# Quadrant attention: masked exponentials cleared on GpSimd, maxima transposed at once, queries and keys in one DMA

## The reference

```python
# layer 0: causal attention with a slope per head
q, k, v = split_heads(layernorm(x) @ W_attn + b_attn)            # 8 x 16 x 512 x 16
s = q @ k.T / (sqrt(16) * temperature) + slope[h] * (j - i)       # ALiBi
p = softmax(where(j <= i, s, -inf))
y = merge_heads(p @ v) @ W_proj + b_proj
# layer 3, second part: attention within sets of tokens, not causal (no mask by position)
p = softmax(q @ k.T / sqrt(16) + set_term(i, j)); y = merge_heads(p @ v) @ W_proj + b_proj
```

## Time and profile before

| | |
|---|---|
| median of 3 runs | 4843.05 us (4834.12 to 4845.9) |
| profiled execution | 4840.89 us, its span 4839.0 us |
| TensorE busy | 4549.0 us, 94% of the span |
| VectorE busy | 2544.5 us, 53% |
| ScalarE busy | 1674.0 us, 35% |
| GpSimd busy | 48.9 us, 1% |
| `score` of layer 0 (L316), 1024 instructions | 210.0 us |
| `score_t` of layer 0 (L323), 1024 | 233.4 us |
| exponentials of layer 0 (L399), 512 | 196.0 us |

### The profile page before, as it was taken

One profiled execution on the slowest core, in us unless ns is written; L12 is line 12 of the kernel. 1 busy time (PEld: TensorE's weight loads), 2 busy tenths in 40 slices (PEclk: granted clock), 3 DMA queues, 4 the chain that ended last, 5 costly groups with the idle time before them and its releaser, 6 DMA issues. The chain is left out here.

```text
span 4839.0 us, 58787 instructions
## 1 busy us (share of the span) xinstructions
PE 4549.0 (94%) x20997; PEld 2683.9 (55%) x20997; DVE 2544.5 (53%) x5867; ACT 1674.0 (35%) x3173; POOL 48.9 (1%) x36
## 2 busy tenths in 40 slices
PE   7999989999999999999999997999797896899997
PEld 3554546756666676666667665666465443333333
DVE  6666653242523325252332523887777776566764
ACT  3444432232222223223232322444342221355554
POOL 0000000000000000000000000000000000000000
PEclk9999999999999999999999998999998898899999
DMA  2000011111111111111111111000000000000001
GB/s 78 14 17 15 15 61 53 70 53 57 66 53 62 61 63 60 53 54 69 62 61 56 49 70 49 1 0 1 0 1 17 1 1 16 19 14 19 14 18 39
DMA packets 47767, 179.15 MB, mean 37 GB/s; under 512 B 12376, under 2 KB 20704, under 8 KB 30184
## 3 DMA queue, kind: packets, MB, share of 16 engines
q1 hardware_dynamic: 47488, 175.35, 10.5%
HBM read 152.76 MB, written 4.19 MB: 32 GB/s over the span
## 5 line engine op out<-in xcount | busy, mean ns | idle before, releaser
L1013 PE MATMUL l_exp_out<-l_w,l_hidden 128*128 128x256 f32 x4096 | 914.0, 384 | 0.3
L1003 PE MATMUL l_hid<-l_xn_t,l_w 128*128 128x512 f32 x2048 | 895.3, 595 | 15.3 <-ACT l_hidden L1132 15.3
L1013 PEld LDWEIGHTS l_exp_out<-l_w,l_hidden 128*128 128x128 f32 x4096 | 782.9, 193 | 118.6 <-issue 9.2
L1132 ACT ACTIVATE l_hidden<-l_hid,l_w 128x512 f32<-128x512 f32 x512 | 350.8, 687 | 1017.5 <-PE l_hid L1003 1017.5
L1003 PEld LDWEIGHTS l_hid<-l_xn_t,l_w 128*128 128x128 f32 x2048 | 390.2, 191 | 490.8 <-issue 466.4
L428 DVE TENSOR_REDUCE l3f_row_max<-l3f_bank 128x1 f32<-128x512 f32 x512 | 328.5, 685 | 178.2 <-PE l3f_bank L316 177.8
L1270 DVE SCALAR_TENSOR_TENSOR l_moe<-l_exp_out,l_gates,l_moe 128x256 f32<-128x256 f32 x256 | 123.6, 483 | 485.3 <-PE l_exp_out L1013 480.6
L399 ACT ACTIVATE l3f_prob_t<-l3f_bank 128x512 f32<-128x512 f32 x512 | 278.0, 595 | 275.3 <-PE l3f_bank L323 275.1
L323 PE MATMUL l3f_bank<-l3f_q_t,l3f_k_t 32*128 32x512 f32 x1024 | 313.8, 640 | 1.4 <-ACT l3f_prob_t L399 1.3
L425 DVE CUSTOM_DVE_ANT_0 l_masked<-l_bank,l_mask 128x384 f32<-128x384 f32 (+3 forms) x512 | 229.1, 488 | 161.0 <-PE l_bank L316 159.1
L316 PE MATMUL l3f_bank<-l3f_k_t,l3f_q_t 32*128 32x512 f32 x1024 | 301.6, 657 | 8.5 <-DMA l3f_q_t<-l3f_set_rows_q 7.4
(11 more groups left out here) (448 smaller groups left out, 6178.8 us busy)
## 6 DMA issues: line engine op xcount, KB each, us to landing
l_w<-in_w SPq DMA_DIRECT2D x128, 1024.0 KB, 5.0
all_x<-in_x SPq DMA_DIRECT2D x8, 512.0 KB, 11.0
l_q_t<-l_packed SPq DMA_DIRECT2D x128, 32.0 KB
l_k_t<-l_packed SPq DMA_DIRECT2D x128, 32.0 KB
l3f_q_t<-l3f_packed SPq DMA_DIRECT2D x128, 32.0 KB
l3f_k_t<-l3f_packed SPq DMA_DIRECT2D x128, 32.0 KB
out_x<-all_x SPq DMA_DIRECT2D x8, 512.0 KB, 5.7
l_hidden<-in_fp4w SPq DMA_DIRECT2D x1, 2304.0 KB
```

What stands on the lines that cost most here:

```text
L1003: ins = nc.tensor.matmul(bank[:, :], w1[:, e % 2, c, f * P:(f + 1) * P], xn_t[:, c, :], start=c == 0, stop=c == CT - 1)
L1013: ins = nc.tensor.matmul(bank[:, 0:C], hidden[:, e % 2, f, j * P:(j + 1) * P], w2[:, e % 2, f, :], start=f == 0, stop=f == HF - 1)
L1132: hid.empty(nc.scalar.activation(hidden[:, e % 2, f, :], bank[:, :], ACT.Relu, bias=w[:, B1][:, e * HF + f:e * HF + f + 1]), (e, f))
```

## The change

1. Layer 0 drops `diagonal`. GpSimd clears the masked exponentials in `prob_t` with `affine_select`, one instruction for two heads (256 elements per partition), two per step. `prob_t` gets a third buffer, and the values follow two steps later in layer 0 (LAG 2), still one in layer 3. So that no exponential above the diagonal grows too large, four spare rows of the slots (`halves`) add -1e30 where the query lies in the first half of a 128-block and the key in the second.
2. The maxima lie densely in `row_max`, so one transpose gives 16 rows of 128. ScalarE copies them, negated, into `max_rows`, and SP writes them into the `MAX_ROW` rows of `q_t` with four DMAs. `centre` is gone. AHEAD grows from 5 to 8; the transpose comes at t % 4 == 1 instead of 3.
3. `q_t` and `k_t` are one tensor `qk_t`, and one DMA per head moves both; the set rows of layer 3 likewise. SP now goes through the steps, with moves at i = 6, 8, 12 and 0 of the next.
4. Some work moves: the transposes of x from i = 3 to 2, the first query and key projections from 5 and 6 to 4 and 5, set rows from 2 to 3, in layer 0 the transposes and copies of y one step later and `yt` from 4 to 5.
5. In layer 3 the copy of the register tokens' queries is four plain copies, and the `channel` mask is gone. Clearing `row_max` at the start is gone in both.

The diff, cut to its core:

```diff
-    AHEAD = TJ + 1
+    AHEAD = 2 * TJ
...
+        self.causal, self.parts, self.flow, self.LAG = causal, parts, flow, 2 if causal else 1
+        self.qk_t = a.sb("qk_t", [P, 2, G, T])
+        self.q_t, self.k_t = self.qk_t[:, 0], self.qk_t[:, 1]
+        self.row_max, self.max_rows = a.sb("row_max", [P, 2, TJ * HPG]), a.sb("max_rows", [TJ * HPG, 2, P])
+        self.prob_t = a.sb("prob_t", [P, self.LAG + 1, HPG, T])
...
+    def move(self, sp, b, g):
+        u, first = g // 2, g % 2 * HPG
+        self.flow.wait_emptied(sp, ("q", b, u))
+        self.flow.wait_emptied(sp, ("k", b, u))
+        for s in range(HPG):
+            sp.dma_start(self.qk_t[s * SLOT:s * SLOT + D, :, g, :],
+                         self.packed[(first + s) * D:(first + s + 1) * D, :, u, :]).then_inc(self.moved[g], 16)
+
+    def move_maxima(self, sp, t):
+        g = self.group_of_maxima(t)
+        if g is not None:
+            self.flow.wait_emptied(sp, ("mx", g))
+            for qt in range(TJ):
+                sp.dma_start(self.q_t[self.MAX_ROW::SLOT, g % G, qt * P:(qt + 1) * P],
+                             self.max_rows[qt * HPG:(qt + 1) * HPG, g % 2, :]).then_inc(self.max_moved, 16)
...
-        qt = self.wave_order[i % TJ]
+        qt = TJ - 1 - (w - self.AHEAD) % TJ if self.causal else i % TJ
...
+    def group_of_maxima(self, t):
+        g, i = divmod(t + self.AHEAD - 1, TJ)
+        return g - 1 if i == 0 and 0 <= g - 1 < B * G else None
+
+    def group_of_sums(self, t):
+        g, i = divmod(t - self.LAG - TJ + 1, TJ)
+        return g if i == 0 and 0 <= g < B * G else None
...
             for s in range(HPG):
-                flow.wait_emptied(pe, ("t", u, s))
+                if not self.causal:
+                    flow.wait_emptied(pe, ("t", u, s))
+                elif s % 2 == 0:
+                    pe.wait_ge(self.selected, 2 * u + s // 2 + 1)
...
-            for j in range(TJ):
-                ins = nc.tensor.transpose(bank[:, j * P:(j + 1) * P], self.row_max[:, g % 2, j].rearrange("p s r -> p (s r)"), ident)
-            flow.fill(ins, ("mx", g))
+            flow.fill(nc.tensor.transpose(bank[0:TJ * HPG, 0:P], self.row_max[:, g % 2, :], ident), ("mx", g))
...
             if t % TJ == 0:
-                flow.wait_emptied(pe, ("mx", t // TJ))
+                pe.wait_ge(self.max_moved, 16 * TJ * (t // TJ + 1))
...
-        if 0 <= t < n:
-            diagonal(0)
-            diagonal(1)
-        if 0 <= t - 1 < n:
-            values(t - 1)
-        if t % TJ == TJ - 1 and 0 <= t + 1 < n:
-            maxima((t + 1) // TJ)
+        if 0 <= t - self.LAG < n:
+            values(t - self.LAG)
+        if self.group_of_maxima(t) is not None:
+            maxima(self.group_of_maxima(t))
...
-            diagonal(2)
-            diagonal(3)
...
+        g = self.group_of_maxima(t)
+        if g is not None:
+            if g >= 2:
+                act.wait_ge(self.max_moved, 16 * TJ * (g - 1))
+            bank = flow.wait_filled(act, ("mx", g))
+            flow.empty(nc.scalar.activation(self.max_rows[:, g % 2, :], bank[0:TJ * HPG, 0:P], ACT.Copy, scale=-1.0), ("mx", g))
...
+    def gpsimd(self, nc, pool, t):
+        for s in (0, 2):
+            for h in (s, s + 1):
+                self.flow.wait_emptied(pool, ("t", t, h))
+            block = self.prob_t[:, t % (self.LAG + 1), s:s + 2, 0:P]
+            nc.gpsimd.affine_select(block, block, [[0, 2], [1, P]], ALU.is_ge, 0.0, 0, -1).then_inc(self.selected, 1)
...
# layer 0, SP
+            sp.wait_ge(halves_ready, 1)
+            for s in range(HPG):
+                rows = slice(s * SLOT + att.MAX_ROW + 1, s * SLOT + att.MAX_ROW + 1 + TJ)
+                for g in range(G):
+                    sp.dma_start(att.qk_t[rows, :, g, :], halves).then_inc(halves_moved, 16)
             sp.dma_start(w[:, WK.stop:BQ.start], w_dram[:, WK.stop:BQ.start]).then_inc(w_loaded, 16)
             for b in range(FIRST, B):
                 load_x(sp, b)
+            for t in TIMES:
+                b, i = divmod(t, att.STEPS)
+                att.move_maxima(sp, t)
...
+                if i in MOVES:
+                    g = MOVES.index(i)
+                    tile = b + 1 if g < G - 1 else b
+                    if 0 <= tile < B:
+                        if tile:
+                            att.wait_group_over(sp, tile - 1, g)
+                        att.move(sp, tile, g)
+                        sp.dma_start(att.q_t[att.MAX_ROW::SLOT, g, :], alibi_dram[0][att.MAX_ROW::SLOT, g, :]).then_inc(att.moved[g], 16)
```

## The result

The changed kernel takes 4826.7 us (median of 20 runs, 4813.6 to 4841.5); the kernel before takes 4841.4 in runs taken beside it. The ratio is 0.9969 with a 95% interval of 0.9961 to 0.9976: 14.6 us faster, where 47 were forecast. The sign was right and more than two thirds of the gain are missing. The time lies inside the range that was given, but only in the part that was kept open for the rivals: the forecast's own range ended at 4812. The profiled span went from 4839.0 to 4825.5 us, 13.5 less, so this execution can be used to say where.

What follows compares the result with a forecast made beforehand. TensorE, busy throughout, was taken as the bound. Terms 44 + 10 + 22 - 10 - 14 - 4 - 1.5 gave 46.5, say 47 us gained: 4795 us; own range 4773 to 4812, with rivals 4772 to 4832.

Steps and rivals of the forecast that it cites:

- Masks: Layer 0: dropping the mask matmuls on TensorE saves 5.5 us per item, a gain of 44 us for eight.
- Rival D: Waits for exponentials replace the mask pairs; only first pairs (27) and maxima (22) remain, less 29: 4821 us. Chance 0.06.
- The held `score_t(3)`: Second half-step of 512 columns waits for an exponential; later values cover 0.3 us in 32 steps, a gain of 10 us.
- Maxima: Both attention stages: one transpose instead of four, 0.22 us instead of 0.58, a gain of 22 us.
- New waits: Half-steps directly following others, and added copies: 1.0 us per item in layer 0, 0.2 in layer 3, a loss of 10.
- The start of layer 0: Three more score waves first, later second projections, 16 small DMAs ahead of the loads: a loss of 14 us, bounds 4 and 22.
- Layer 3's start: Three waves and two projections later (+11), first wave 5 to 7 us earlier: a loss of 4 us.
- Selection on GpSimd: Layer 0: selections of 0.8 us (0.4 to 1.6), two per step, hidden by the values' lag: costs nothing.
- Rival A: GpSimd becomes the bound in layer 0; at 3.1 us per selection the kernel takes 5042 us. Chance 0.07.
- Rival C: VectorE and GpSimd exclude each other: 2 us per item plus bank waits, 30 us in all, 4825 us. Chance 0.07.
- DMAs: Moves of maxima, queries and keys land before TensorE needs them, tightest 5.1 of 6.8 us: costs nothing.
- rival B: Group 0's move comes late if doubled DMA size doubles issue time: 7 and 18 us, so 4820 us. Chance 0.11.

## Why the prediction was right or wrong

**What bounds the kernel**: right before, no longer quite after. The forecast took over from "TensorE is busy throughout" that VectorE, needed for 47 of 75 us, could not set the pace. Over an item it doesn't; in single steps it does (1.27 us of standing still in step 4). This is the step that failed first: an average over the item was taken for a statement on each wait, so VectorE's waits stood at nothing in the sum. Per item of layer 0 the forecast's terms came out so: masks 3.4 instead of 5.5, selections -0.6 instead of nothing, maxima 1.5 instead of 1.4, the held `score_t(3)` and the new waits together -0.6 instead of +0.2. That makes 3.8 where 7.1 were forecast.

**Masks** (forecast 44 us): the term that was most wrong. Taken out of the kernel before they are worth 34 us (4.30 per item), in the changed kernel 27 (3.42). The first pairs gave their 0.21 wherever nothing else was late. The step that failed is that each pair was counted at its full length wherever it stood. Of the second pair 0.05 moved into the full-array operation behind it and 0.03 into a wait for an exponential. And masks filled waits that stayed: in steps 11 and 14 of the kernel before, in steps 4 and 14 of the changed one wholly, in 5, 9, 11 and 13 by 0.19 each. Rival D, given 0.06, says that waits take the place of the masks, and its figure of 27 us is what the changed kernel shows. But that is luck: it named exponentials, and most of these waits are VectorE's.

By the Trainium skill ("TensorEngine Tiling (Array Packing)", Key Properties) a change of tiling mode drains the array. The trace agrees in that part of the gap passed on to the next full-array operation when the masks went (1.87 to 1.92 us). For the maxima the forecast's further use of that rule, that a fixed 0.1 would go too, wasn't borne out.

**The held `score_t(3)`** (forecast 10): in the 512-column steps 0.18 came off (1.46 to 1.28), in step 4 only once VectorE's stall was taken away, 0.21 stayed (0.1 was forecast), and three of the four 384-column steps lost 0.22 each (0.07 with the masks back, since the first pair covers the rest). Net nothing, at best. The step that failed looked at the step that gains by the lag and not at the one whose cover it takes.

**Maxima** (forecast 22): right. 0.20 us each instead of 0.58, so 0.38 instead of 0.36 saved.

**New waits** (forecast 10 us, 1.0 per item): in layer 3 right (item 80.86). In layer 0 the direct half-steps from step 6 to 7 cost 0.6 where 0.4 was said (1.68 us for what are 0.65 and 0.43 elsewhere), and the waits of step 4 (1.3), of step 7 (0.44) and of the 384-column half-steps weren't foreseen. The change moved dx behind the gate product in front of the longest wave; the diff shows it, and the forecast never listed what VectorE does between two waves.

**The start of layer 0** (forecast 14, bounds 4 and 22; measured 22.1). The first wave comes 8.3 us later where 5 was taken: 5.6 of it on SP's queue, near the 5, and 2.7 between the last issue and the wave, which the forecast left out. The rest was 13.8 instead of 8.8: the projections 7.1 us instead of 3, with no overlap, and the waves 6.7 (what remains) instead of 5.8.

**Layer 3's start** (forecast 4 between -3 and 12): 0.8. **Ends**: 1.7 us gained at the end where a loss of about 0.7 was expected.

**Selection on GpSimd** (forecast nothing): a selection takes 0.46 us on average, near the lower end of the 0.4 to 1.6 given, and GpSimd spends its time waiting:

```profile
L433 POOL TENSOR_SCALAR_AFFINE_SELECT l_prob_t<-l_prob_t 128x256 f32<-128x256 f32 x256 | 117.9, 462 | 521.4 <-ACT l_prob_t L402 521.4
```

Rival A is refuted. Rival C is true for 4.5 us, not 30: VectorE was held up in dx and the mixing (dx 796 against 684 ns), and not in the maxima (688 against 687). The means hide two cases: of the two dx of an item one takes 0.68 us, with 0.12 us of a selection beside it, and the other 0.91, with 0.37 beside it. It goes the other way too: between 100 and 600 us 24 of the 224 selections took 0.65 to 1.31 us, 200 took 0.41. The Trainium skill ("SBUF — State Buffer", Who interferes with whom) says that a VectorE instruction with two SBUF inputs contends with a GpSimd instruction that reads SBUF. The trace agrees for dx and the mixing. In the same section the Trainium skill lists `tensor_scalar` among the operations that can contend too, in a mode that uses two ports. The normalisation of x, such an operation on one tile in SBUF with two scalars of a row, got longer as well (470 against 408 ns); whether it ran in that mode no run here shows. The lag that was to be the cover of the selections is worth only 1 us per item.

**DMAs** (forecast nothing): right. Four moves of queries and keys in one took 2.53 us, 0.63 each, where those of half the size took 0.61, and no wait for them shows in the running part; rival B is refuted.

## What to carry to other kernels

Work on the bounding engine that stands in front of a wait is worth only what the wait leaves: before pricing a removed instruction, list for each place it is taken from who comes last when it is gone, and look at every step of the period, since a lag or a reordering that helps one step takes its cover from another. An engine that is busy for 64% of a period still sets the pace where long operations queue in front of short ones that free a buffer; moving one 1.2 us operation by a few steps brought 11 us, a quarter of what the whole change was forecast to bring. And a longer software pipeline is paid at each start: DMAs issued ahead of the first loads and work moved behind the first wave cost 15 us here, and reordering alone gave them back.

## What the runs showed of the hardware

Removing a matmul pair of another shape left 0.05 us of its 0.12 behind, in the next full-array operation. VectorE's operations on SBUF alone got longer beside GpSimd's selections (dx 684 to 796 ns, mixing 746 to 822), the maxima with an input in PSUM didn't (687 to 688), and a selection beside VectorE took up to 1.31 us. GpSimd's selection of 128 x 256 elements in place took 0.46 us on average and 0.41 undisturbed, a third of its operation on two inputs of twice the elements (1.55 us). Issues on SP for DMAs from SBUF depended little on their size: in layer 0's running part four in a row took mostly 2.2 us for the maxima (2 KB each), 2.4 to 2.5 for 32 KB and 2.5 to 2.6 for 64 KB, and the sixteen of 16 KB at the start took 0.69 each.
